# Decoder kernel, last stage: the softmax sums of the full rounds move from TensorE's ones product and VectorE's reciprocal to ScalarE

## What is computed

```python
# _L1_attn_ref: 16 heads of 32, causal  ("P" in the kernel)
scores = einsum('bhqd,bhkd->bhqk', q, k) * HD ** (-0.5)
scores = where(causal, -1e9, scores)
a = softmax(scores, axis=-1)
ctx = einsum('bhqk,bhkd->bhqd', a, v)
out = einsum('bsd,ed->bse', ctx, w_o)
# _L1_xattn_ref: one head of 512 over the 256 cached tokens and the 256 own ("C")
# _L1_ffn_ref: a gate picks one of 16 heads for each token ("H"); then 16 query heads
#              attend causally to the one picked key and value head ("A"), like the above
```

## Time and profile before

| | |
|---|---|
| median of 3 runs (lowest to highest) | 2128.2 us (2126.52 to 2128.36) |
| the profiled execution, span | 2127.3 us |
| busy: TensorE, VectorE, GpSimd, ScalarE | 97%, 53%, 27%, 24% |
| tail stage | from 1179.94 us to the end |
| rounds 3 to 7, each | 111.16 us |

### The profile page before, as it was taken

How to read it: one execution, slowest core, us unless ns; L and a number is a source line. 1 busy time by engine, 2 the same in 40 slices (tenths; PEclk the granted TensorE clock), 3 DMA queues, 4 the chain that set the end, 5 groups by cost and what they waited for, 6 DMA issues and landing times. The chain is left out here.

```text
span 2127.3 us, 32323 instructions
## 1 busy us (share of the span) xinstructions
PE 2057.7 (97%) x13439; PEld 1194.6 (56%) x13439; DVE 1128.4 (53%) x1731; ACT 518.8 (24%) x791; POOL 580.5 (27%) x548
## 2 busy tenths in 40 slices
PE   7899999999999999999999999999999999999996
PEld 5444444334444557556566655766666666666664
DVE  2567777567777744122222334364646464736567
ACT  2445555440000121101011122122222222222211
POOL 2222222128999600111110312022222222121122
PEclk9999999999999999999999999999999999999998
DMA  5101111205111147321211602100010101000000
GB/s 161 48 1 55 55 56 45 87 38 210 40 43 44 35 156 277 126 65 65 65 65 55 222 3 99 50 31 21 17 44 1 60 1 41 1 31 12 1 11 21
DMA packets 66237, 130.81 MB, mean 61 GB/s; under 512 B 6480, under 2 KB 19920, under 8 KB 66096
## 3 DMA queue, kind: packets, MB, share of 16 engines
q1 hardware_dynamic: 45968, 77.49, 11.1%
q10 hardware_dynamic: 14448, 32.64, 4.3%
q0 software_dynamic: 5680, 18.62, 3.0%
HBM read 97.40 MB, written 41.81 MB: 65 GB/s over the span
## 5 line engine op out<-in xcount | busy, mean ns | idle before, releaser
L1033 PE MATMUL conv_conv<-kv,toep 128*128 128x512 f32 x576 | 247.6, 592 | 0.3 <-POOL kv L1067 0.3
L2615 DVE RECIPROCAL tail_inv<-tail_ring 128x256 f32<-128x256 f32 x63 | 110.7, 1757 | 188.8 <-PE tail_ring L1935 188.3
L1623 PE MATMUL moe_gu_ps<-gu,xT_tile 128*128 x608 | 192.4, 459 | 0.0
L1033 PEld LDWEIGHTS conv_conv<-kv,toep 128*128 128x128 f32 x576 | 109.4, 190 | 139.0 <-issue 129.6
L1067 POOL TENSOR_TENSOR kv<-vT,cT 128x512 f32<-128x512 f32 x128 | 147.0, 1172 | 15.8 <-PE conv_conv L1033 12.0
L2302 POOL TENSOR_TENSOR tail_rstd_x<-tail_rstd_x,const_minus_half 128x2 f32<-128x2 f32 x31 | 21.8, 702 | 469.6 <-DVE tail_rstd_x L2577 469.6
L1623 PEld LDWEIGHTS moe_gu_ps<-gu,xT_tile 128*128 128x128 f32 x608 | 112.3, 190 | 66.5 <-issue 17.8
L2310 POOL TENSOR_SCALAR_AFFINE_SELECT tail_expT<-tail_expT 128x1024 f32<-128x1024 f32 x64 | 71.5, 1119 | 242.1 <-ACT tail_expT L2394 242.0
L2603 DVE TENSOR_REDUCE tail_negtop<-tail_scores 128x4 f32<-128x1024 f32 x64 | 78.2, 1221 | 95.6 <-PE tail_scores L1886 95.4
L594 POOL TENSOR_SCALAR_AFFINE_SELECT front_expT<-front_expT 128x2048 f32<-128x2048 f32 x32 | 64.3, 2008 | 199.1 <-ACT front_expT L649 199.1
L1604 POOL DMA_INDIRECT xg<-x_after,tokens x37 | 35.0, 947 | 282.3 <-PE moe_xT_ps L1618 255.2
(11 more groups left out here) (394 smaller groups left out, 3912.2 us busy)
## 6 DMA issues: line engine op xcount, KB each, us to landing
toep<-toeplitz SPq DMA_DIRECT2D x32, 320.0 KB, 2.9
y_slots<-moe_y ACTq DMA_DIRECT2D x39, 256.0 KB, 2.0
gu<-in_L_ffn_gate_up_proj SPq DMA_DIRECT2D x5, 1408.0 KB, 12.5
toeplitz<-filt_rows SPq DMA_DIRECT2D x8, 768.0 KB
front_e<-in_ctx SPq DMA_DIRECT2D x8, 512.0 KB, 4.7
toeplitz<-filt_rows SPq DMA_DIRECT2D x16, 256.0 KB
x_after<-x SPq DMA_DIRECT2D x8, 512.0 KB, 5.0
tail_x<-x_after SPq DMA_DIRECT2D x8, 512.0 KB, 3.7
```

The lines of the kernel that those rows point to most:

```text
L1033: ins = pe.matmul(bank, toep[p][:, mat * P:(mat + 1) * P], kv[p][:, c].rearrange("p b j i -> p (b j i)"), start=n == 0, stop=n == len(PART ...
L1623: ins = pe.matmul(gu_ps[:, s % 2, h, 0:HID], (xT if s else mid.xT_first)[:, c, :], wgu[c][:, e, h * HID:(h + 1) * HID], start=c == 0, stop ...
L2615: link.after(dve.reciprocal(inv[c % 2][:], bank[:, S:2 * S]))
```

## The change

It concerns eleven units, P of sequences 2 to 7 and A of sequences 0 to 4 (`normal`). For them `maxima` no longer drains `scores`; ScalarE waits for the maxima (`topped`) and runs `sums`: for each head and half an exponential of the masked scores with minus the maximum as its bias, whose results go to a scratch region and whose sum goes to `esum`; the last one drains `scores`. After the fourth group `take_logs` takes the logarithm of the sums, and `split_top` subtracts it from `negtop`: so the transposed exponentials come out normed. `causal` leaves out its addition, `weigh` its ones product, and `mix` is a copy. The other five units keep their way. For all sixteen units the shift is now split into three bf16 parts, in another layout, and `picks` takes the place of `pick16`, with twelve selections instead of eight. In the loop the order moves: ScalarE's queue gets the sums between its copies, TensorE's shift goes behind a projection of values, and both transposes of C go ahead of P's first transposed score.

```diff
-WEDGE = 96
+WEDGE = 128
...
-        split = st.sb("split", [P, NT, 4, 2, NG], BF16)
-        pick16 = st.sb("pick16", [P, 4, P], BF16)
+        split = st.sb("split", [P, NT, 4, 32], BF16)
+        picks = st.sb("picks", [P, 4, P], BF16)
...
+        normal = [unit for r in range(2, B) for unit in (("A", r - 3), ("P", r)) if unit[1] >= 0]
+        PARTS = [(t, g) for t in (1, 0) for g in range(4)]
...
+                    if not bare:
+                        for g in range(4):
+                            ins = pe.matmul(bank[32 * g:32 * g + 32, S:2 * S].rearrange("p (n q) -> p n q", q=P), ones32[:],
+                                            e[:, 1:3, g] if last else last_rows(kind, b, c)[:, :, g], start=False, stop=not last,
+                                            skip_group_check=True)
...
                     if P_: cols("P", "k", p, 1, wide["wk"])
+                    if P_: rows("P", "v", p, 0, xT[p % 2], wide["wv"])
                     if A_: shift("A", a)
-                    if P_: rows("P", "v", p, 0, xT[p % 2], wide["wv"])
+                    if C_: turn("C", "x4", c)
                     if A_: scoreT("A", a, 0)
-                    if C_: turn("C", "x4", c)
...
+                    if H_: rows("H", "v", h, 0, xT[h % 2], wide["gv"])
                     if P_: shift("P", p)
-                    if H_: rows("H", "v", h, 0, xT[h % 2], wide["gv"])
+                    if C_:
+                        for t in range(NT):
+                            cross_turn(c, t)
                     if P_: scoreT("P", p, 0)
...
-                    if kind == "A" and b == B - 1:
+                    if (kind, b) == ("A", B - 1) or (kind, b) in normal:
                         return
...
+                def sums(kind, b, c):
+                    key = (kind, "S", b, c)
+                    act.wait_ge(topped, place(kind, b, c) + 1)
+                    for t, g in PARTS:
+                        h = 4 * c + g
+                        ins = act.activation(hidden[:, g, keys_of(t)], scores[:, g, keys_of(t)], ACT.Exp, bias=negtop[:, t, h:h + 1],
+                                             accum_out=esum[:, t, h:h + 1])
+                    ins.then_inc(quads.drained_sem(key), 1)
+
+                def take_logs(kind, b):
+                    key = (kind, "S", b, NC - 1)
+                    act.wait_ge(quads.drained_sem(key), quads.count(key))
+                    act.activation(logs[:], esum[:], ACT.Ln).then_inc(logs_ready, 1)
...
+                act.preload_act_table_set("natural_log_exp_and_others")
...
+                    sums("P", p, 0)
+                    if C_: take(("C", "q", c, 1), pair(qx, 1))
+                    sums("P", p, 1)
+                    if C_: cross_exp(c, 0)
+                    sums("P", p, 2)
+                    if C_: cross_exp(c, 1)
+                    if H_: take_turned("H", h)
+                    sums("P", p, 3)
+                    take_logs("P", p)
...
+                    if (kind, b) in normal:
+                        for t in (1, 0):
+                            ins = dve.tensor_reduce(negtop[:, t, heads_of(c)], scores[:, :, keys_of(t)], AX_X, ALU.max, negate=True)
+                        ins.then_inc(topped, 1)
+                        return
...
                 def split_top(kind, b):
...
+                    link.after(dve.tensor_copy(part(0), by_strip(whole)))
+                    link.after(dve.tensor_tensor(by_strip(rest), by_strip(whole), part(0), ALU.subtract))
+                    link.after(dve.tensor_copy(part(1), by_strip(rest)))
+                    dve.tensor_tensor(part(2), by_strip(rest), part(1), ALU.subtract).then_inc(split_ready[kind], 1)
...
                     bank = filled((kind, "W", b, c))
+                    if (kind, b) in normal:
+                        dve.tensor_copy(mixedT[:, c, :], bank[:, 0:S]).then_inc(ring.drained_sem((kind, "W", b, c)), 1)
+                        return
```

More of the change, by code:

```diff
@@ L1759, in tail_stage @@
         ones32 = st.sb("ones32", [P, HD])
-        expT = [st.sb(f"expT{p}", [P, 4, 4, P]) for p in range(3)]
+        expT = st.sb("expT", [P, 12, 4, P])
+        hidden = expT[:, 9:12].rearrange("p n g q -> p (n g q)").rearrange("p (g s) -> p g s", g=4)
+        esum, logs, total, rest = (st.sb(n, [P, NT, NG]) for n in ("esum", "logs", "total", "rest"))
         xneg = st.sb("xneg", [P, NT])
@@ L1892, in shift @@
                     for n, t in enumerate((1, 0, 1)):
-                        ins = pe.matmul(bank[:, n * P:(n + 1) * P], split[:, t].rearrange("p r a h -> p (r a h)"),
+                        ins = pe.matmul(bank[:, n * P:(n + 1) * P], split[:, t].rearrange("p r h -> p (r h)"),
                                         consts["ident_bf"][:], start=True, stop=True)
@@ L1904, in scoreT @@
                         s = slice(32 * g, 32 * g + 32)
-                        pe.matmul(bank[:, g, 0:3 * P], pick16[s, c], shiftT[s].rearrange("p n q -> p (n q)"),
+                        pe.matmul(bank[:, g, 0:3 * P], picks[s, c], shiftT[s].rearrange("p n q -> p (n q)"),
                                   start=True, stop=False, skip_group_check=True)
@@ L1931, in weigh @@
                         for g in range(4):
[L1932 to L1936, removed]
+                            ins = pe.matmul(bank[32 * g:32 * g + 32, lo:S].rearrange("p (n q) -> p n q", q=P), v(kt, g),
+                                            e[:, 0:1, g] if kt else e[:, 1:3, g], start=kt == 0, stop=bare and kt == 1, skip_group_check=True)
+                    if not bare:
[3 more added lines that the diff above has]
+                                            skip_group_check=True)
                     if last:
@@ L2485, in _ @@
                     P_, C_, H_, A_ = p is not None, c is not None, h is not None, a is not None
+                    if P_: take_turned("P", p)
+                    for j in range(2):
+                        if A_: sums("A", a, 2 * j)
+                        if P_: take(("P", "q", p, j), pair(qT["P"], j), SCALE)
+                        if A_: sums("A", a, 2 * j + 1)
+                        if P_ and j == 0: take(("P", "k", p, j), pair(kT["P"], j))
+                    if A_: take_logs("A", a)
                     if P_:
-                        take_turned("P", p)
-                        for j in range(2):
-                            take(("P", "q", p, j), pair(qT["P"], j), SCALE)
-                            take(("P", "k", p, j), pair(kT["P"], j))
+                        take(("P", "k", p, 1), pair(kT["P"], 1))
+                        take(("P", "v", p, 0), v_p[:, 0, :])
                     if A_: take_shift("A", a)
-                    if P_: take(("P", "v", p, 0), v_p[:, 0, :])
+                    if C_: take_turned("C", c)
                     if A_: exps("A", a, 0)
-                    if C_: take_turned("C", c)
                     if P_: take(("P", "v", p, 1), v_p[:, 1, :])
```

82 lines of the change are left out of this document (49 added, 33 removed).

## The result

The changed kernel takes 2166.9 us (median of four runs, 2160.7 to 2168.7) against 2128.3: 1.0179 times as long, 95% interval 1.0164 to 1.0195. The forecast was 2165, in a range of 2150 to 2188, slower with a chance of 0.93. The profiled execution's span is 38.7 us longer than before's.

A forecast was written before the change was run, and what follows sets the result against it. TensorE's queue was taken to bound the full rounds. Five rounds +27.6, round 2 +3.2, start +2.3 and +0.1, last splits +0.6, clock +3: +36.8 on 2127.3 us, forecast 2165 after allowing for the median, range 2150 to 2188.

The forecast's parts named there:

- The cycle: Score to score of one unit, through maxima on VectorE and sums on ScalarE: at least 6.58 us.
- the middle one of three values: A group's sums on ScalarE: 3.41 us, between 2.52 (accumulator reads free) and 4.04 (each read holding the engine).
- Rivals 1: Each accumulator read holds ScalarE its full 0.19 us: group 4.04, cycle 7.21, kernel 2187 us; chance 0.15.
- 3 (G below 2.3): Kernel gets faster, if a group's sums on ScalarE (time G) take under 2.3 us; chance 0.05.
- Waits a round: New TensorE waits before scores in a full round: 9.9 us, less 4.36 removed, so +5.5 a round.
- What is removed: The ones product on TensorE, 0.545 us in each of 44 full-round groups: 24.0 us, 4.36 a round of 8.
- Round 2: Only P there, without A's products between: three waits, 5.4 us, less 2.18 removed: +3.2 us.
- The clock: TensorE's clock falls to half once a full round, at the 2.2 us wait: 5 x 0.65, +3 us.
- Rival 2: TensorE's clock falls at most waits of 1.8 us too, 12 to 18 us more: about 2180 us; chance 0.17.
- The shift: TensorE's shift behind the fourth score does not wait; A's is covered by 0.3 to 0.4 us, P's by more.
- Start and end: Outside full rounds: turn of x3 +2.3 us, wider wedge +0.1, longer splits of the last two units +0.6.
- Rival 4: Logarithm and exponentials share no table, so each unit pays two loads of 1.28 us; hardly a chance.

The follow-up runs named there:

- e2: The changed kernel with only the four 256-column sums of each group, the 128-column ones left out: 2119.5 us.
- e8: The changed kernel with the eight ACTIVATEs of each group kept but without accumulators, full-round attention left unnormed: 2137.8 us.
- e3: The changed kernel with the eight sums of each group made twice, the second after the first have ended: 2328.5 us.
- e5: The changed kernel with TensorE's work in A's phase reordered, one and a half projections instead of one between A's scores, ScalarE's queue to match: 2140.0 us.
- e1: The kernel before, without the ones product in the eleven full-round units and with a copy in place of reciprocal and product: 2109.0 us.
- e10: The changed kernel without sums and logarithm, with ones product, GpSimd addition and reciprocal kept in all units: 2129.4 us.
- e6: The changed kernel with GpSimd's root of x3 and its fetch ahead of the twelve selections: 2162.7 us.
- e4: The changed kernel with one maximum over a group's four heads, two ACTIVATEs without accumulator, VectorE adding up from SBUF afterwards, and some order moved: 2116.8 us.
- e7: e4 with the edit of e6 and ScalarE's copy of the turned x5 ahead of C's second exponentials: 2116.6 us.
- e9: e4 with the edit of e6 and VectorE's maximum for C's second exponentials ahead of its additions for P's third group: 2114.7 us.

## Why the prediction was right

**The cycle.** Right, and shown by e2, e8, e3 (its length) and e5 (what fills it). 6.58 was forecast, 6.50 and 6.59 measured. The group takes 3.33, not 3.41: the middle one of three values that I weighed was the right one, since a read costs only up to the next start (e8). By the Trainium skill's prices (ScalarE: Activation LUTs, section "What ACT_TABLE_LOAD costs") the eight without their reads would take 2.78 from start to start, an estimate; e8's rows have 2.44 (1660.83 to 1663.27, or 2.60 to the last one's end), and my 2.52 from the rows was nearer. Rivals 1 (reads hold the engine) and 3 (G below 2.3) are out by that.

**Waits a round.** Forecast 9.9, measured 8.90. A's: 5.83 forecast, 5.43 measured, the first 0.2 shorter. P's: 1.13, 1.13, 1.80 forecast, 0.86, 0.96, 1.65 measured: I had reckoned TensorE's work in the first two of P's gaps without the ones product at 5.45; it is 5.56 in e1. The rest is the cycle (6.50 in two of the three) and the 0.07 told below.

**What is removed.** The step that failed in size: 44 x 0.545 = 24.0 is 44 x 0.43 = 19.0 (e1). I had taken the time from the ones product's start to the next start, and not seen that the piece ahead ends sooner when it stands there.

**What I had not counted.** The piece ahead of a wait runs 0.07 longer from start to start: 3.72 instead of 3.65 for a projection (the row at 1675.29), the way it is where nothing follows it at once. Six times a round, 0.42. By these terms a round without a fall of the clock is 111.04 (e10) - 3.46 (e1) + 8.90 + 0.42 = 116.90, against 116.94 measured. My +5.5 against +5.8 a round was so near by luck: two errors of 0.9 and 1.0 stood against each other.

**Round 2.** +3.2 forecast, +3.8 measured, 0.4 of it the clock (98.9 in e6, where it did not fall there; 99.3 here, 95.5 before).

**The clock.** One fall a round at 0.65, 3 us, was forecast. In the changed kernel it fell once in each of rounds 2, 3 and 6 and twice in round 4, not in 5 and 7, and in rounds 3 to 7 it cost 588.6 - 5 x 116.94 = 3.9, with round 2 4.3. Rival 2 (most waits) is out. The Trainium skill (TensorE: Matmul & The Clock Gate, the rules at its end) warns of idle gaps between bursts, and means longer ones than any wait of these rounds; here the clock fell behind some of the waits of 1.65 to 2.03, and not behind all. A fall behind a wait, round 3:

```profile
1437.92 0.44 PE L123 MATMUL tail_scores<-const_wedge,const_ident_bf 32*32 32x256 bf16 x16 [2.03 <-ACT tail_expT L2434]
1438.29 1.24 PE L1910 MATMUL tail_scores<-tail_kT_a,tail_qT_a 32*128 32x256 f32 x8
1439.31 0.65 PE L1913 MATMUL tail_scores<-tail_kT_a,tail_qT_a 32*128 32x128 f32 x8
```

The score takes 1.97 instead of 1.12 until the projection starts (1439.89), and that 0.85 is lost; the projection's own loss of 0.7 is taken back by the next wait, 1.03 instead of 1.74. The first fall of round 4 hits only the projection and costs nothing, since the next score would have waited anyway; its second stands behind P's last wait, where nothing waits any more to take it back (the turn takes 1.09 in round 5):

```profile
1556.82 5.41 PE L191 MATMUL tail_ring<-tail_xT,tail_wk 128*128 128x256 f32 x16
...
1617.53 0.33 PE L123 MATMUL tail_scores<-const_wedge,const_ident_bf 32*32 32x256 bf16 x16 [1.65 <-ACT tail_expT L2434]
...
1618.66 1.82 PE L1875 MATMUL tail_ring<-const_ident,tail_x 128*128 128x128 f32 x8
```

Rounds 3, 4 and 6 lost 0.84, 1.52 and 1.53, the last also behind P's last wait. I had put five falls of 0.65 at A's longest wait; only two stood there, and they cost 0.84 and nothing. That the sum came near (3 against 4.3) is luck.

**The shift** had no wait, as forecast, nor had C's transposes ahead of P's first transposed score. A's shift had less cover than I reckoned: in round 5 it starts 8.12 behind its score, not 8.4, and VectorE's split ends 0.25 before it. In e3, with 3.4 more, both wait.

**Start and end.** 2.3 forecast for the turn of x3, 1.7 measured. The selections took longer by less:

```profile
1186.30 10.23 POOL L2359 TENSOR_SCALAR_AFFINE_SELECT tail_picks<-tail_picks 128x512 bf16<-128x512 bf16 x12
1196.50 0.72 POOL L2333 TENSOR_TENSOR tail_rstd_x<-tail_rstd_x,const_minus_half 128x2 f32<-128x2 f32 x1
```

Counted from the start of the stage, as the 1.7 is, they end 3.3 later than in the earlier trace rows, not 3.9; and the root, which waited for VectorE before, starts 2.65 later, not 3.3. The wedge's 0.1 can't be seen. The last two splits cost 0.34 each, 0.7, as forecast (0.6); the stretch behind the loop is 0.9 longer.

**The sum:** 1.7 + 3.8 + 32.8 (five rounds) + 0.9, less 0.5 because the stage began earlier, is +38.7 against +36.8 forecast. Rival 4, table loads in each unit, did not happen: the logarithm takes 0.23, and the whole stage has one table load, 1.28 us at 1179.36.

## What to carry to other kernels

Where one buffer goes round between engines, add up its cycle (fill, use by each reader, handover) and compare it with what the filling engine has to do between two fills; load and busy share say nothing. A reader that is added to the cycle can be paid for by work put between the fills (e5, -5 us a round), by fewer instructions in the reader, or by letting it leave the buffer early and doing the rest elsewhere (e4 does both). And the price of a piece in a pipelined queue is that from the start of the piece ahead of it to the start of the one behind, with and without: taken from its own start it was a quarter too high here.

## What the runs showed of the hardware that I had not expected

- A matmul piece hands over later when it is followed by another kind of piece or by nothing: 0.68 or 0.79 for the products by values, 3.65 or 3.72 for a projection.
- The read of an accumulator lasts 0.19 to 0.24 in its row and costs 0.09, also eight times in a row.
- Equal waits don't give equal clocks. Rounds 3 to 7 of the changed kernel have the same work and, where it doesn't fall, the same waits to 0.01; yet the clock fell in rounds 3, 4 and 6 and not in 5 and 7, once behind a score at full speed, in the projection after it (the row at 1556.82). With waits of up to 1.3 (e8), or of 0.97 and less (e1, e2, e4, e7, e9, e10), it stayed at 1.00 in every round from 3 to 7; in e5, with 1.66 as the longest, it fell in round 3 and not in 4 to 7. Which wait brings a fall stays open.
- What a fall costs depends on what it hits: 0.84 us on a score, 1.5 on pieces with no wait behind them, nothing on a projection that ends before a wait. In e6 the clock shows 0.99 in rounds 4 and 7 as well, and they last 116.95 and 116.97, no more than a round without a fall.
